# Fourteen drives by token instead of seven in a state-space scan, and rows of B spread ahead of other work on TensorE

## The chip, the cores and the metric

The kernel runs on one core of a Trainium2 chip. The metric is the device time of one launch in microseconds (us). A core has five engines with a queue of instructions each: TensorE (PE; its weight loads are listed as PEld), VectorE (DVE), ScalarE (ACT), GpSimd (POOL) and SyncE (SP), which here only starts DMA transfers. The engines wait for each other by semaphores, and each works its own queue strictly in order. PSUM, the memory that TensorE writes, has 8 banks of 128 x 512 f32.

## The reference

The input is x, 2 sequences of 1024 tokens with 128 values. The layer is a Mamba block with a residual and a layer norm, then a mixture of 8 experts (top 2, limited capacity) with a residual and a layer norm. The part around the change is the recurrence of the Mamba block, with 256 channels d and 16 states n:

```python
xz = x @ W_in;  x_in, z = split(xz, 2)
u  = silu(causal_conv4(x_in) + conv_b)
B, C = split(u @ W_x, 2)                    # 16 values each per token
dt = softplus(u @ W_dt + b_dt)
h[t] = exp(dt[t] * A) * h[t-1] + (dt[t] * u[t]) * B[t]     # state [256, 16]
y[t] = sum_n h[t, :, n] * C[t, n]
y = (y + u * D) * silu(z);  x1 = layernorm(x + y @ W_out)
# then: logits = x1 @ w_g, top 2 of 8 experts, ranks by a running count,
# rows gathered by expert, gelu(rows @ c_fc) @ c_proj, weighted, added back,
# second layernorm
```

## The kernel before

The 2048 tokens are cut into four chunks of 512 (q = 0 to 3), and a chunk has 16 units, one for each state n. A unit is numbered U = 16 q + n, 0 to 63. Channels lie on the 128 partitions in two halves d = 0 and 1. For a unit the kernel needs:

- the decay exp(dt * A[n]), made by ScalarE into PSUM banks 4 and 5 (`decays`, line 1067), once the scan of the unit before has read the bank;
- the drive dt * u * B[n]. In the usual way TensorE spreads row n of B over all partitions by a matmul with a selector (`spread_b`, line 648) into one of two banks, and VectorE multiplies it with dtu = dt * u (`drives`, line 1633);
- the scan itself, two instructions on VectorE, one per half (`scan`, line 1662);
- the product with C on GpSimd (`multiply`, line 1425), and its sum over n, added up in PSUM by TensorE (`add_to_y`, line 678 in chunks 0 to 2, where the sum is a transpose in accumulation, line 673 in chunk 3).

Seven units, listed in `TURNED` (line 54), get their drive in another way, by token: dtu, transposed beforehand so that tokens lie on the partitions (`dtu_t`), is scaled by a column of the transposed B (`b_t`) in four instructions of ScalarE (`drive_by_token`, line 1099, queued three units ahead), and eight 128 x 128 transposes of TensorE (`turn_drive`, line 664, two groups of four) bring it back to channels in the two banks that rows of B use. VectorE then has no multiplication for that unit: its scan reads PSUM directly. The decay of such a unit goes to SBUF in one instruction (`decay_sb`, line 1062). Four of the seven lie in chunk 0 (units 4, 7, 10, 14), three in chunk 3 (53, 57, 60).

State has a ring of three buffers, so the scan of unit U waits for the product of U - 3. VectorE runs each unit as: scan of half 0, the drive of the next unit, scan of half 1, then small work of the routing. Each engine's order is written out by hand. TensorE's loop (lines 820 to 880) runs for unit U: `spread_b` of the drive that VectorE makes during U (that of U + 1, or of U + 2 if U + 1 is turned), the sums of U - 2, transposes of a turned unit, and then a piece of work ("job") for another chunk: convolution, the B/C and dt projections of the next chunk, z, and for the chunk before y transposed, the output projection (`project_out`, lines 757 to 774) and the counting of experts. Jobs share PSUM banks 6 and 7 in the fixed order of `JOBS` (line 391); a job waits until ScalarE has taken the one before it in its bank. In unit n = 3 of chunks 1 to 3 TensorE waits until VectorE has gated the y of the chunk before (`gate`, line 1669), and then starts the new sum (`start_y`, lines 622 to 633). `share` on VectorE (line 1750) waits for a denominator of the routing which GpSimd makes (line 1481).

After unit 63 come the routing of the last chunk, the scatter of rows to their experts, the experts and the second norm; nothing in that part is touched.

Of the kernel before, what the change touches and what calls it, by code (L numbers as in the profile page):

```python
# [14 lines left out]
P = 128  # L15
# [38 lines left out]
TURNED = (4, 7, 10, 14, 53, 57, 60)  # L54
# [32 lines left out]
def layer_program(nc, x, W_in, channel_values, conv_rows, W_x, W_dt, A_log, W_out, w_g, c_fc, c_proj, out):  # L87
    with ExitStack() as ctx:
# [64 lines left out]
        b_t = sb("b_t", [P, TPC, D_STATE])  # L153
# [232 lines left out]
        def last_tile(e, s):  # L386
# [5 lines left out]
                ("z2a", 1), ("z2b", 0), ("wout", 1), ("wcat", 0),  # L392
                ("bc2", 1), ("dt2a", 0), ("dt2b", 1), ("y0a", 0), ("y0b", 1), ("out0a", 0), ("out0b", 1), ("conv3a", 0), ("rank0", 1),
                ("conv3b", 0),
                ("bc3", 1), ("dt3a", 0), ("dt3b", 1), ("y1a", 0), ("y1b", 1), ("out1a", 0), ("out1b", 1), ("rank1", 1),
# [137 lines left out]
        def _(pe):  # L533
# [199 lines left out]
            def turn_w_out():  # L733
                bank, made = job_bank("wout")
                pe.wait_ge(w_late_loaded, 32)
                pe.wait_ge(center_made, 1)
                for k in range(DT):
                    nc.tensor.transpose(psum[:, bank, k * P:(k + 1) * P], w_out_sb[:, k, :], ident[:, :])
                nc.tensor.matmul(psum[:, bank, DT * P:DT * P + N_EXP], center[:, 0:D_MODEL], w_g_sb[:, :], start=True, stop=True).then_inc(made, 1)
# [17 lines left out]
            def project_out(q, pair):  # L757
                for d in "ab":
                    turned, before = JOB[f"y{q}{d}"]
                    pe.wait_ge(w_taken[turned], before + 1)  # L760
                if q == 0:
                    turned, before = JOB["wcat"]
                    pe.wait_ge(w_taken[turned], before + 1)
                bank, made = job_bank(f"out{q}{'ab'[pair]}")
                b, c = divmod(q, NCH)
                for j in range(2 * pair, 2 * pair + 2):
                    for k in range(DT):
                        nc.tensor.matmul(out_tile(q, j), y_chan[:, k, j * P:(j + 1) * P], w_cat[:, k, :], start=(k == 0), stop=False)
                    t = PAD + c * CH + j * P
                    last = nc.tensor.matmul(out_tile(q, j), x_chan[:, b, t:t + P], center[:, :], start=False, stop=True)  # L770
                if q == 1 and pair == 0:
                    pe.wait_ge(bc_rows_ready, NQ)
                    turn_b(b_t_psum(bank, B_AT))
                last.then_inc(made, 1)
# [45 lines left out]
            for U in range(LAST + 1):  # L820
# [5 lines left out]
                if U in TURNED:  # L826
                    turn_drive(U, 1)
                elif U >= 1 and U - 2 not in TURNED and drive_beside(U):
                    spread_b(drive_beside(U))
# [10 lines left out]
                if U - 1 in TURNED:  # L840
                    spread_b(drive_beside(U + 1))
                if U + 1 in TURNED:
                    turn_drive(U + 1, 0)
                if q == 2 and n in (12, 14):
                    dtu_job(3, (n - 12) // 2)
                if q == 0:
# [6 lines left out]
                    elif n <= 6:  # L853
                        dt_job(1, n - 5)
                    elif n <= 10:
                        conv_job(2, (n - 7) // 2, range((n - 7) % 2 * 2, (n - 7) % 2 * 2 + 2))
                    elif n <= 12:
                        z_job(2, n - 11)
                    elif n == 13:
                        turn_w_out()  # L860
                    elif n == 15:
                        center_w_out()
                else:
# [108 lines left out]
        def _(act):  # L972
# [59 lines left out]
            def take_b(rows):  # L1032
                act.wait_ge(b_turned, 1 if rows is first_b else 2)
                if rows is not first_b:
                    act.wait_ge(drive_t_ready, TPC * sum(T < D_STATE for T in TURNED))
                nc.scalar.activation(b_t[:, :, :].rearrange("p j n -> p (j n)"), rows, ACT.Copy).then_inc(b_t_ready, 1)

            first_b = b_t_psum(B_BANK, 0)
            take_b(first_b)
# [47 lines left out]
            def drive_by_token(U):  # L1087
                q, n = divmod(U, D_STATE)
                before = TURNED.index(U)
                act.wait_ge(drive_turned, DT * before)  # L1090
                if q == 0:
                    act.wait_ge(dtu_t_ready, 1)
                    act.wait_ge(b_t_ready, 1)
                else:
                    bank, done = JOB["t3b"]
                    act.wait_ge(w_taken[bank], done + 1)
                    act.wait_ge(b_t_ready, 2)
                for j in range(TPC):
                    nc.scalar.activation(drive_t[:, j, :], dtu_t[:, j, :], ACT.Copy, scale=b_t[:, j, n:n + 1]).then_inc(drive_t_ready, 1)
# [66 lines left out]
            def take_out(q, pair):  # L1166
                act.wait_ge(logits_copied, 2 * q + pair + 1)
                rows, taken = job_made(f"out{q}{'ab'[pair]}")
                if q == 1 and pair == 0:
                    take_b(rows[:, B_AT:B_AT + TPC * D_STATE])  # L1170
# [44 lines left out]
            def take_w_out():  # L1215
                rows, taken = job_made("wout")
                nc.scalar.activation(w_out_t[:, :, :].rearrange("p k m -> p (k m)"), rows[:, 0:DT * P], ACT.Copy).then_inc(w_out_t_ready, 1)
                nc.scalar.activation(center[:, D_MODEL:WIDE], rows[:, DT * P:DT * P + N_EXP], ACT.Copy).then_inc(taken, 1)
# [7 lines left out]
            for U in range(LAST + 1):  # L1226
# [12 lines left out]
                for T in TURNED:  # L1239
                    if T - AHEAD.get(T, 2) == U:  # L1240
                        decays(T)
                    if T - 3 == U:
                        drive_by_token(T)
                if q == 2 and n in (13, 15):
# [22 lines left out]
                if q == 0:  # L1267
# [17 lines left out]
                    elif n == 14:  # L1285
                        take_w_out()
                else:
# [76 lines left out]
        def _(gp):  # L1364
# [80 lines left out]
            def times_u(q):  # L1445
                gp.wait_ge(dt_ready, DT * (q + 1))
                if q >= 2:
                    gp.wait_ge(drive_ready, drive_number(D_STATE * (q - 1)))
                    gp.wait_ge(dtu_turned, 1)
# [522 lines left out]
```

## Time and profile before

| | us |
|---|---|
| median of 3 runs | 391.63 (391.55 to 392.54) |
| profiled execution, its own time | 392.27 |
| its span, first to last instruction | 390.5 |
| VectorE busy | 290.3 |
| TensorE busy | 289.5 |
| GpSimd busy | 265.7 |
| ScalarE busy | 201.1 |

The slices of the page show the engines' busy share in tenths over 40 equal pieces of 9.8 us, and the clock that TensorE was granted (9 is full speed, 2.4 GHz; 5 is half, 1.2 GHz):

```profile
PE   8896798669686768675854799766089999998700
DVE  2699889999999999969999999995212333334566
ACT  2858987946635694753564647661302223332405
POOL 4506789968778899887889886897520555556622
PEclk9999999998788857969565699999579999999955
```

The first two slices are the start. Slices 3 to 27 are the 64 units, and what follows is routing of the last chunk and the experts.

### The profile page before, as it was taken

To read this page: it belongs to the slowest core of one execution; us is meant where nothing else is said; L and a number is where in the kernel's file an instruction comes from. 1 tells how busy PE (TensorE), PEld (TensorE's weight loads), DVE (VectorE), ACT (ScalarE), POOL (GpSimd) and SP (SyncE) were. 2 spreads that over 40 slices of the span, in tenths; PEclk is the share of its full clock that TensorE was granted. 3 is DMA by queue.
4 is the path that set the end of the run, shared out by engine and by line. 5 is a ranking of instruction groups with operands and counts; after the bars stand their busy time and mean duration, and the time that the engine had idled before them with its cause. 6 is when DMAs were issued, how large, how long until landed. Compare 5 with 4: busy or idle time off the path is not lost. (4 is left out here: it accounts for less than half of the span.)

```text
span 390.5 us, 4954 instructions
## 1 busy us (share of the span) xinstructions
PE 289.5 (74%) x1493; PEld 205.0 (53%) x1493; DVE 290.3 (74%) x436; ACT 201.1 (51%) x398; POOL 265.7 (68%) x226
## 2 busy tenths in 40 slices
PE   8896798669686768675854799766089999998700
PEld 6455455537564454564542464324088888887600
DVE  2699889999999999969999999995212333334566
ACT  2858987946635694753564647661302223332405
POOL 4506789968778899887889886897520555556622
PEclk9999999998788857969565699999579999999955
DMA  7061087462333254221212231001053434332773
GB/s 221 12 220 54 2 274 257 127 216 88 144 107 134 81 163 146 68 70 51 104 60 74 82 114 55 1 14 41 31 143 82 116 114 125 93 89 71 212 223 112
DMA packets 35786, 42.90 MB, mean 110 GB/s; under 512 B 3862, under 2 KB 26331, under 8 KB 35760
## 3 DMA queue, kind: packets, MB, share of 16 engines
q1 hardware_dynamic: 32336, 37.38, 30.8%
q0 software_dynamic: 2304, 4.24, 3.3%
q10 hardware_dynamic: 1120, 0.97, 0.9%
q8 instruction: 12, 0.20, 0.2%
q14 instruction: 14, 0.11, 0.1%
HBM read 30.11 MB, written 12.79 MB: 110 GB/s over the span
## 5 line engine op out<-in xcount | busy, mean ns | idle before, releaser
L1425 POOL TENSOR_TENSOR product<-state,c_wide 128x1024 f32<-128x1024 f32 x64 | 149.6, 2344 | 45.0 <-DVE state L1662 29.0
L1067 ACT ACTIVATE psum<-dt,a_neg 128x512 f32<-128x512 f32 x110 | 75.1, 687 | 79.3 <-DVE state L1662 77.9
L678 PE MATMUL psum<-ident,product 128*128 128x128 f32 x384 | 61.4, 313 | 33.3 <-POOL product L1425 33.3
L678 PEld LDWEIGHTS psum<-ident,product 128*128 128x128 f32 x384 | 51.2, 162 | 49.5 <-POOL product L1425 46.1
L1633 DVE TENSOR_TENSOR drive<-dtu,psum 128x1024 f32<-128x1024 f32 x57 | 68.3, 1198 | 7.3 <-PE psum L648 7.1
L1662 DVE TENSOR_TENSOR_SCAN state<-psum,carry,drive 128x512 f32<-128x512 f32 x58 | 72.2, 1268 | 0.2
L1662 DVE TENSOR_TENSOR_SCAN state<-psum,drive 128x512 f32<-128x512 f32 x56 | 66.7, 1210 | 2.5 <-ACT psum L1067 2.3
L1547 POOL DMA_INDIRECT result_rows<-state,result_at x30 | 30.3, 1011 | 40.4 <-DVE state L1876 33.1
L1501 POOL DMA_INDIRECT slot_rows<-sent,scatter_at x32 | 32.9, 1029 | 10.6 <-issue 6.8
L904 PE MATMUL psum<-product,fc_sb 128*128 128x320 f32 x128 | 36.1, 435 | 1.1 <-DVE product L1844 1.1
L1841 DVE TENSOR_SCALAR tags<-c_wide 128x10 f32<-128x10 f32 x8 | 1.3, 164 | 43.1 <-PE psum L893 43.1
L1326 ACT ACTIVATE u<-psum 128x640 f32<-128x640 f32 x16 | 11.3, 704 | 38.3 <-PE psum L904 37.2
L673 PE MATMUL psum<-product,ident 128*128 128x512 f32 x60 | 28.3, 599 | 2.7 <-POOL product L1425 2.6
L904 PEld LDWEIGHTS psum<-product,fc_sb 128*128 128x128 f32 x128 | 22.8, 190 | 11.3 <-issue 2.2
L1326 ACT ACTIVATE z_tok<-psum 128x640 f32<-128x640 f32 x16 | 11.3, 704 | 27.6 <-PE psum L904 18.9
L648 PE MATMUL psum<-bc_parts,selector 128*128 128x512 bf16 x57 | 24.5, 432 | 0.7 <-DVE drive L1633 0.7
L723 PE MATMUL psum<-x_chan,w_conv 128*128 128x512 f32 x48 | 23.9, 624 | 1.4 <-ACT sent L1172 1.1
L673 PEld LDWEIGHTS psum<-product,ident 128*128 128x128 f32 x60 | 10.7, 190 | 15.2 <-issue 9.5
L957 PE MATMUL psum<-ident 128*128 128x128 f32 x52 | 8.1, 332 | 10.7 <-DMA slot_rows<-sent,scatter_at 10.7
L578 PE MATMUL psum<-u,w_dt_sb 128*128 128x512 f32 x24 | 13.0, 668 | 3.8 <-ACT bc_parts L1112 2.7
L1876 DVE TENSOR_TENSOR state<-psum,result_weight 128x640 f32<-128x640 f32 x6 | 4.9, 824 | 14.4 <-PE psum L917 14.4
L1551 POOL DMA_INDIRECT late_rows<-state,result_at x10 | 10.6, 1064 | 5.9 <-DVE state L1872 4.1
(256 smaller groups left out, 513.2 us busy)
## 6 DMA issues: line engine op xcount, KB each, us to landing
c_wide<-c_rows SPq DMA_DIRECT2D x32, 512.0 KB, 4.0
slot_rows<-blank SPq DMA_DIRECT2D x8, 325.0 KB, 4.7
c_wide<-slot_rows SPq DMA_DIRECT2D x8, 325.0 KB, 3.3
result_rows<-zeros SPq DMA_DIRECT2D x8, 256.0 KB, 5.0
late_rows<-zeros SPq DMA_DIRECT2D x8, 256.0 KB
fc_sb<-in_c_fc SPq DMA_DIRECT2D x8, 256.0 KB
proj_sb<-in_c_proj SPq DMA_DIRECT2D x8, 256.0 KB
c_wide<-result_rows SPq DMA_DIRECT2D x8, 256.0 KB
```

Source lines behind the costliest of these rows:

```text
L648: nc.tensor.matmul(psum[:, b_bank(U), :], selector[:, n, :], bc_parts[:, q * CH:(q + 1) * CH], start=True, stop=True).then_inc(b_spread, 1)
L673: nc.tensor.matmul(psum[:, Y_BANK + d, :], ident[:, :], product[:, i, d, :], start=False, stop=True, skip_group_check=True).then_inc(summe ...
L678: last = nc.tensor.matmul(y_part(j, d), product[:, i, d, j * P:(j + 1) * P], ident[:, :], is_transpose=True, start=False, stop=True, skip_ ...
L723: last = nc.tensor.matmul(psum[:, bank, :], w_conv[:, k, d * P:(d + 1) * P], x_of(q, k), start=(k == 0), stop=(k == D_CONV - 1))
L904: last = nc.tensor.matmul(psum[:, 2 + 2 * (h % 2) + s, 0:HALF], fc_sb[:, i, h * P:(h + 1) * P], rows_chan[:, i, s * HALF:(s + 1) * HALF], ...
L1067: nc.scalar.activation(psum[:, A_BANK + d, :], dt[:, q % 2, d, :], ACT.Exp, scale=a_neg[:, n:n + 1]).then_inc(decay_ready, 1)
L1326: nc.scalar.activation(hidden[e % 2][:, h, :].rearrange("p (s k) -> p s k", s=2), psum[:, 2 + 2 * (h % 2):4 + 2 * (h % 2), 0:HALF], ACT.Ge ...
L1425: nc.gpsimd.tensor_tensor(product[:, U % PRODUCTS, channels, :], state[:, U % RING, channels, :], wide, ALU.mult).then_inc(product_ready, 1)
L1501: gp.indirect_dma_start(out=slot_rows, out_offset=bass.IndirectOffsetOnAxis(ap=scatter_at[:, k, j:j + 1], axis=0), in_=sent[:, k, j, :], i ...
L1547: gp.indirect_dma_start(out=result_rows, out_offset=bass.IndirectOffsetOnAxis(ap=result_at[:, i, s:s + 1], axis=0), in_=rows_out[:, i, s, ...
L1633: nc.vector.tensor_tensor(drive[:, drive_number(U) % 2, :, :], dtu[:, q % 2, :, :], psum[:, b_bank(U), :].unsqueeze(1).to_broadcast([P, DT ...
L1662: nc.vector.tensor_tensor_scan(state[:, U % RING, d, :], decay, rows, before, ALU.mult, ALU.add).then_inc(scanned, 1)
```

## The change

Fourteen units are turned instead of seven, four each in chunks 0, 1 and 3 and two in chunk 2. `b_t` has two buffers, and B is transposed once per chunk: for chunk 1 in the job of `turn_w_out`, for chunks 2 and 3 in the output projection of the chunk two before. dtu of chunks 1 and 2 is transposed in four new jobs (t1a, t1b, t2a, t2b), taken by ScalarE. On TensorE the spreading of a row of B moves from the head of a unit to behind the sums of the unit before it, ahead of that unit's job; only behind a turned unit it stays at the head. `center_w_out` moves from unit 15 to unit 16. GpSimd's `times_u` gets a wait for the last transposes of dtu.

```diff
-TURNED = (4, 7, 10, 14, 53, 57, 60)
+TURNED = (4, 7, 10, 14, 19, 22, 26, 29, 43, 46, 51, 54, 57, 60)
...
-        b_t = sb("b_t", [P, TPC, D_STATE])
+        b_t = sb("b_t", [P, 2, TPC, D_STATE])
...
-                ("z2a", 1), ("z2b", 0), ("wout", 1), ("wcat", 0),
+                ("z2a", 1), ("z2b", 0), ("wout", 1), ("t1a", 0), ("t1b", 1), ("wcat", 0),
...
-                ("bc3", 1), ("dt3a", 0), ("dt3b", 1), ("y1a", 0), ("y1b", 1), ("out1a", 0), ("out1b", 1), ("rank1", 1),
+                ("bc3", 1), ("dt3a", 0), ("dt3b", 1), ("y1a", 0), ("y1b", 1), ("t2a", 0), ("t2b", 1), ("out1a", 0), ("out1b", 1), ("rank1", 1),
...
@@ turn_w_out, TensorE
+                pe.wait_ge(bc_rows_ready, 2)
+                turn_b(b_t_psum(bank, B_AT))
@@ project_out, TensorE
-                if q == 1 and pair == 0:
-                    pe.wait_ge(bc_rows_ready, NQ)
+                if q <= 1 and pair == 0:
+                    pe.wait_ge(bc_rows_ready, q + 3)
                     turn_b(b_t_psum(bank, B_AT))
@@ the loop over units, TensorE
                 if U in TURNED:
                     turn_drive(U, 1)
-                elif U >= 1 and U - 2 not in TURNED and drive_beside(U):
+                elif U - 1 in TURNED and drive_beside(U):
                     spread_b(drive_beside(U))
...
                 for k in SUMS[q].get(n, []):
                     add_to_y(q * D_STATE + k)
-                if U - 1 in TURNED:
+                if U not in TURNED and U < LAST and drive_beside(U + 1):
                     spread_b(drive_beside(U + 1))
                 if U + 1 in TURNED:
                     turn_drive(U + 1, 0)
+                if q == 2 and n in (6, 7):
+                    dtu_job(2, n - 6)
...
-                    elif n == 15:
+                    elif n >= 14:
+                        dtu_job(1, n - 14)
+                else:
+                    if q == 1 and n == 0:
                         center_w_out()
-                else:
@@ ScalarE
-            def take_b(rows):
-                act.wait_ge(b_turned, 1 if rows is first_b else 2)
-                if rows is not first_b:
-                    act.wait_ge(drive_t_ready, TPC * sum(T < D_STATE for T in TURNED))
+            def take_b(q, rows):
+                act.wait_ge(b_turned, q + 1)
+                if q >= 2:
+                    act.wait_ge(drive_t_ready, TPC * sum(T < D_STATE * (q - 1) for T in TURNED))
...
+                if q == 2 and n in (6, 7):
+                    take_dtu(2, n - 6)
...
                         take_w_out()
+                    if n >= 14:
+                        take_dtu(1, n - 14)
@@ times_u, GpSimd
-                    gp.wait_ge(dtu_turned, 1)
+                    if q == 2:
+                        gp.wait_ge(dtu_turned, 1)
+                    else:
+                        for half in "ab":
+                            bank, before = JOB[f"t{q - 2}{half}"]
+                            gp.wait_ge(w_made[bank], before + 1)
```

## Rows read from the trace of the kernel before

**Rows 1.** Busy time by stretch (chunks 0 to 3, rest): PE, PEld, DVE, ACT, POOL, clock.

```profile
24.00:79.50 55.50, 44.06 (x244) 30.05 (x243) 51.15 (x45) 45.13 (x83) 42.70 (x20) 1.00 0.47 157
79.50:141.50 62.00, 46.02 (x227) 31.27 (x226) 60.61 (x76) 36.63 (x68) 49.32 (x36) 0.83 0.40 129
141.50:205.40 63.90, 44.49 (x228) 33.10 (x227) 58.81 (x77) 36.41 (x80) 54.97 (x42) 0.74 0.26 89
205.40:263.00 57.60, 43.88 (x150) 22.35 (x148) 56.26 (x72) 35.16 (x69) 49.58 (x39) 0.85 0.18 58
263.00:390.50 127.50, 90.69 (x579) 75.75 (x579) 50.47 (x151) 34.79 (x78) 59.27 (x58) 0.88 0.39 111
```

**Rows 2.** Waits of VectorE, 24 to 264 us: total, times, longest.

```profile
DVE drive L1633 <- PE psum L648: 7.1, 8, 3.5
DVE state L1662 <- ACT psum L1067: 2.3, 5, 0.7
```

**Rows 3.** Groups by line and form: busy us, mean ns, idle before.

```profile
L1633 DVE TENSOR_TENSOR drive<-dtu,psum 128x1024 f32<-128x1024 f32 x57 | 68.3, 1198 | 7.3 <-PE psum L648 7.1
...
L648 PE MATMUL psum<-bc_parts,selector 128*128 128x512 bf16 x57 | 24.5, 432 | 0.7 <-DVE drive L1633 0.7
...
L1099 ACT ACTIVATE drive_t<-dtu_t,b_t 128x256 f32<-128x256 f32 x28 | 11.9, 494 | 0.0
...
L664 PE MATMUL psum<-ident,drive_t 128*128 128x128 f32 x56 | 8.2, 275 | 0.1
```

**Rows 4.** VectorE in order of time, chunks 1 to 3: start, us, idle before.

```profile
107.27 1.22 DVE L1633 TENSOR_TENSOR drive<-dtu,psum 128x1024 f32<-128x1024 f32 x1 [0.70 <-PE psum L648]
108.41 2.45 DVE L1662 TENSOR_TENSOR_SCAN state<-psum,carry,drive 128x512 f32<-128x512 f32 x2
...
150.43 1.22 DVE L1633 TENSOR_TENSOR drive<-dtu,psum 128x1024 f32<-128x1024 f32 x1 [0.63 <-PE psum L648]
...
175.34 1.22 DVE L1633 TENSOR_TENSOR drive<-dtu,psum 128x1024 f32<-128x1024 f32 x1 [3.52 <-PE psum L648]
...
198.40 0.18 DVE L1750 RECIPROCAL denom<-denom 128x4 f32<-128x4 f32 x1 [0.45 <-POOL denom L1481]
...
222.65 1.22 DVE L1633 TENSOR_TENSOR drive<-dtu,psum 128x1024 f32<-128x1024 f32 x1 [0.95 <-PE psum L648]
```

**Rows 5.** The same of chunk 0: a drive behind turned unit 7.

```profile
54.38 1.22 DVE L1633 TENSOR_TENSOR drive<-dtu,psum 128x1024 f32<-128x1024 f32 x1 [0.42 <-PE psum L648]
```

**Rows 6.** All engines in order of time, around unit 19.

```profile
87.24 0.58 ACT L1111 ACTIVATE bc_sb<-psum 128x512 f32<-128x512 f32 x1
...
88.36 3.11 PE L578 MATMUL psum<-u,w_dt_sb 128*128 128x512 f32 x4 [1.91 <-ACT bc_parts L1112]
...
91.69 2.34 PE L632 MATMUL psum<-diag_d,u 128*128 128x128 f32 x16
...
96.03 1.22 DVE L1633 TENSOR_TENSOR drive<-dtu,psum 128x1024 f32<-128x1024 f32 x1 [0.18 <-PE psum L648]
```

**Rows 7.** GpSimd in order of time, units 25 to 27.

```profile
118.19 2.37 POOL L1425 TENSOR_TENSOR product<-state,c_wide 128x1024 f32<-128x1024 f32 x1 [1.38 <-issue]
...
130.63 0.20 POOL L1481 TENSOR_TENSOR denom<-denom,others 128x4 f32<-128x4 f32 x1
```

**Rows 8.** All engines in order of time, units 39 to 41.

```profile
170.02 1.97 PE L678 MATMUL psum<-ident,product 128*128 128x128 f32 x8 [2.22 <-POOL product L1425]
...
174.91 0.39 PE L648 MATMUL psum<-bc_parts,selector 128*128 128x512 bf16 x1
...
175.14 1.04 PE L678 MATMUL psum<-ident,product 128*128 128x128 f32 x8
...
177.83 2.36 POOL L1425 TENSOR_TENSOR product<-state,c_wide 128x1024 f32<-128x1024 f32 x1 [3.25 <-issue]
```

**Rows 9.** TensorE in order of time, units 51 and 52.

```profile
217.08 1.97 PE L754 MATMUL psum<-ident,z_tok 128*128 128x128 f32 x8 [5.17 <-DVE z_tok L1669]
...
218.84 3.56 PE L625 MATMUL psum<-u,diag_d 128*128 128x512 f32 x4
```

More of the change, by code:

```diff
@@ L1029, in _ @@
                     nc.scalar.activation(bc_sb[:, :], psum[:, B_BANK + 1, :], ACT.Copy).then_inc(bc_rows_ready, 1)
-            def take_b(rows):
-                act.wait_ge(b_turned, 1 if rows is first_b else 2)
-                if rows is not first_b:
-                    act.wait_ge(drive_t_ready, TPC * sum(T < D_STATE for T in TURNED))
-                nc.scalar.activation(b_t[:, :, :].rearrange("p j n -> p (j n)"), rows, ACT.Copy).then_inc(b_t_ready, 1)
-            first_b = b_t_psum(B_BANK, 0)
-            take_b(first_b)
+            def take_b(q, rows):
+                act.wait_ge(b_turned, q + 1)
+                if q >= 2:
+                    act.wait_ge(drive_t_ready, TPC * sum(T < D_STATE * (q - 1) for T in TURNED))
+                nc.scalar.activation(b_t[:, q % 2, :, :].rearrange("p j n -> p (j n)"), rows, ACT.Copy).then_inc(b_t_ready, 1)
+            take_b(0, b_t_psum(B_BANK, 0))
             copy_x(3)
@@ L1090, in drive_by_token @@
                 act.wait_ge(drive_turned, DT * before)
+                act.wait_ge(b_t_ready, q + 1)
                 if q == 0:
                     act.wait_ge(dtu_t_ready, 1)
-                    act.wait_ge(b_t_ready, 1)
                 else:
-                    bank, done = JOB["t3b"]
-                    act.wait_ge(w_taken[bank], done + 1)
-                    act.wait_ge(b_t_ready, 2)
+                    job_taken(f"t{q}a")
+                    job_taken(f"t{q}b")
                 for j in range(TPC):
-                    nc.scalar.activation(drive_t[:, j, :], dtu_t[:, j, :], ACT.Copy, scale=b_t[:, j, n:n + 1]).then_inc(drive_t_ready, 1)
+                    nc.scalar.activation(drive_t[:, j, :], dtu_t[:, j, :], ACT.Copy, scale=b_t[:, q % 2, j, n:n + 1]).then_inc(drive_t_ready, 1)
             def job_made(name):
@@ L1168, in take_out @@
                 rows, taken = job_made(f"out{q}{'ab'[pair]}")
-                if q == 1 and pair == 0:
-                    take_b(rows[:, B_AT:B_AT + TPC * D_STATE])
+                if q <= 1 and pair == 0:
+                    take_b(q + 2, rows[:, B_AT:B_AT + TPC * D_STATE])
                 tiles = slice(TPC * q + 2 * pair, TPC * q + 2 * pair + 2)
@@ L1217, in take_w_out @@
                 nc.scalar.activation(w_out_t[:, :, :].rearrange("p k m -> p (k m)"), rows[:, 0:DT * P], ACT.Copy).then_inc(w_out_t_ready, 1)
+                take_b(1, rows[:, B_AT:B_AT + TPC * D_STATE])
                 nc.scalar.activation(center[:, D_MODEL:WIDE], rows[:, DT * P:DT * P + N_EXP], ACT.Copy).then_inc(taken, 1)
```

## The prediction

> **What bounds the kernel now.** I read the page's slices first, then the busy time of each chunk, then the waits of VectorE, then the order of time where it waits. The slices show VectorE at nine tenths in nearly all of slices 3 to 27, which are the 64 units. The stretches [rows 1] say how close: VectorE is busy 51.15 of 55.5 us in chunk 0, 60.61 of 62.0 in chunk 1, 58.81 of 63.9 in chunk 2 and 56.26 of 57.6 in chunk 3. The 127.5 us behind them are not touched by the change and only shift. GpSimd comes next and is the engine to watch: 49.32 of 62.0 in chunk 1, but 54.97 of 63.9 in chunk 2. What VectorE waits for inside the units is little: 7.1 us for TensorE's spread rows of B, 2.3 us for decays [rows 2]. So there are two things to win, work on VectorE and the 7.1 us, and about 9 us of GpSimd idle time in chunk 2 to win it in.
>
> **Part 1: drives leave VectorE.** Unit 53 goes back to the usual way, eight units leave it, net seven: four in chunk 1 (19, 22, 26, 29), two in chunk 2 (43, 46), one in chunk 3. A drive lasts 1.20 us [rows 3] but overlaps its neighbour: the one that starts at 107.27 is followed by a scan at 108.41, 1.14 us later, a wait before it included or not [rows 4]. I take 1.13. Upper end: 7 x 1.13 = 7.9 us. Lower end: see the first rival.
>
> **Part 2: the same work on ScalarE and TensorE.** ScalarE gets 7 x 4 = 28 scalings more, at 11.9 / 28 = 0.43 us each beside each other [rows 3] 1.7 us per unit, 12 us in all, and four dtu copies, two copies of B. It is busy 36.63 of 62.0 and 36.41 of 63.9 us in chunks 1 and 2 [rows 1], and its jobs lie between two decays. The decays of a unit must be there 3.4 us (two scans, one drive) after the last ones could start, so a job of 1.7 us fits beside 1.3 us of decays, and behind a turned unit there is a whole unit more, because the decay of the unit after it needs only the scan before it. I count nothing for ScalarE; if that cover is gone the price is a few tenths at a unit, up to 7 x 0.5 = 3.5 us. TensorE gives a spread (0.43) and takes eight transposes (8.2 / 56 = 0.15 each, 1.2 per unit) [rows 3]: 7 x 0.7 = 5 us, and some 5 us for the dtu and B transposes. It has 16 and 19 us idle in chunks 1 and 2 [rows 1], so it costs only where something is queued behind.
>
> **Part 3: the spread in front of the job.** Behind the sums of unit U TensorE now spreads B for the drive of U + 2. It needs the drive of U done (it shares a bank), and that ends about when the product of U - 2 does, on which the sums wait, so I charge no new wait. What it skips are jobs. In chunks 1 to 3 five waits are long [rows 4, 6]: 0.18 (behind two sums and `start_y`), 0.70 (behind an output projection), 0.63 (behind the B/C projection), 3.52 (behind sums and an output projection) and 0.95 (behind y transposed and `start_y`). The waits of 0.70 and 0.63 go whole. Those of 0.18 and 0.95 don't, since `start_y` and not a job is ahead of them. In chunk 0 nothing goes: its waits, such as the 0.42 at 54.38 [rows 5], stand behind turned units, where the spread stays at the head of the unit, behind the job.
>
> The wait of 3.52: the sums start at 170.02 and wait for GpSimd, last 1.77 at the low clock, then comes the projection until the spread at 174.91 [rows 8]. In the new order the spread runs at 171.8 and the drive can start at 172.2 instead of 175.34, 3.1 us earlier. But the projection and the new job t2b (four transposes at the low clock, 1.0 us) are now behind it, and the spread after them waits for both: 171.8 + 0.4 + 1.0 + 2.9 (the projection) + 1.0 (sums, as at 175.14) + 0.4 = 177.5 at the low clock, 176.5 if the clock rises at 174.4 as it did. VectorE would want its drive at 175.8 (172.2 + drive + two scans). So 0.7 us comes back as a wait, and chunk 2 keeps 2.3 to 2.4; I take 2.3.
>
> **Part 4: chunk by chunk.**
> Chunk 1, unit 19. This is where it is tight. TensorE's queue is now: dt projection of half b, second group of transposes of 19, gate wait, `start_y`, two sums, and only then the row for the drive of 21. The projection waits for ScalarE's bc rows, which end later by the new decay and scaling (87.24 [rows 6], about 1.0 us later). Before, `start_y` began at 91.69 and the drive at 96.03; VectorE now wants that drive 1.1 us earlier, and TensorE has it at best at 95.6 (clock high) and at worst at 98 (the projection at the low clock lasts 3.11, the transposes 1.0). Between +0.4 and -2; I take -0.5. Units 22, 26 and 29 give 1.13 each, and 0.70 from part 3: 4.1, less 0.5 is 3.6. Now the cap: from the product of unit 25 at 118.19 GpSimd works without a gap (times_u, score, products) until the denominator at 130.63 [rows 7], for which VectorE's `share` in unit 28 waits. This chain of 12.6 us starts earlier only by what was won until unit 25, which is -0.5 + 1.13 + 0.70 = 1.3; the gain of 26 is lost there, that of 29 comes behind it. Chunk 1 gives 1.3 + 1.13 = 2.4 us.
> Chunk 2: 0.6 + 2.3 = 2.9 us until unit 41. Then the same chain of GpSimd; in this chunk VectorE already waits 0.45 us for it [rows 4], so unit 43's 1.13 is lost, and unit 46's comes behind it: 1.1. GpSimd can follow, its gap of 3.25 us at 177.83 [rows 8] is the twin of the 3.52. Chunk 2 gives 4.0 us.
> Chunk 3: one drive less, but the turned unit is now 51, the one with `start_y`. There TensorE is bound by the gate: 8 transposes from 217.08, `start_y` from 218.84 until 222.4 [rows 9], both at the low clock, then the row. VectorE reaches it one drive earlier and waits 2.1 instead of 0.95: 0 us, and up to 2 if the clock is high there (`start_y` 3.56 then takes half).
>
> Sum: 2.4 + 4.0 + 0 = 6.4 us. The profiled execution took 392.27 us (span 390.5), so 385.9; it lies 0.64 above the median 391.63, which gives **385.2 us**.
>
> **The rivals.**
> *Every turned unit brings its own wait.* For it: chunk 0 has four turned units and 55.5 - 51.15 = 4.35 us of VectorE idle [rows 1], about 1.09 per unit, nearly what a drive costs; chunk 1 without any has 1.39. Against it: in chunk 0 ScalarE is busy 45 of 55 us, in chunks 1 and 2 it is 36 of 62. The time: 7 x (1.13 - 1.09) = 0.3 and 0.70 + 0.63 + 2.3 of the reorder, 3.9 less: 387.7.
> *Nothing else takes the place.* All 7.9 us, and all waits for TensorE of chunks 1 to 3, 0.18 + 0.70 + 0.63 + 3.52 + 0.95 = 6.0: 377.7. For it: GpSimd has 12.7 and 8.9 us of room. Against it: the gap-free chain of GpSimd [rows 7].
> *The low clock makes TensorE the bound* (the slower side). A sum takes 1.97 us at the low clock and 1.04 at the high one [rows 8]. In chunks 1 and 2 TensorE is busy 46.02 + 44.49 = 90.5 us at a mean clock of 0.83 and 0.74, about 71 us at the full clock, and some 8 more now. At the low clock throughout that is 158 us in stretches that lasted 126: sums arrive late, the ring of state stops VectorE. It decides from a mean clock of 79 / 126 = 0.63 down; at 0.60 the two stretches last 132 instead of 126, at 396 to 398 us, less what chunk 3 gives. For it: the clock already fell from 0.83 to 0.74 as gaps of 2 to 3 us before the sums grew, and a matmul of 512 columns is replaced by transposes. Against it: TensorE gets more work and shorter gaps.
> The Trainium skill (TensorE: Matmul & The Clock Gate, Part 4: PE-mode transpose) says that transposes don't count as busy for the clock in the way matmuls do. The trace leans that way: chunks 1 and 2, where the sums are transposes, have 0.83 and 0.74, chunk 3 with matmul sums 0.85 [rows 1]; but chunk 0, full of transposes between projections, has 1.00. By that rule the clock would fall with this change and the third rival's time would hold; I don't follow it, because the trace's low stretches go with idle gaps.
>
> **How the numbers follow.** The forecast 0.50, nothing takes its place 0.12, each unit its own wait 0.20, the low clock 0.12, and 0.06 for a mixture that ends at no change. The range: 380.5 (part of the second rival's way) to 391.0 (all new waits of unit 19 and ScalarE's 3.5 us, 6.4 - 1.5 - 3.5 = 1.4 less, and a margin), which leaves out most of the full and of the slow case. Changes under 0.3%, 1.2 us, can't be told from none. Faster 0.50 + 0.12 + 0.18 = 0.80, same 0.06 + 0.02 = 0.08, slower 0.12.
>
> **What would show it.** Right: VectorE's wait at the drive of unit 41 falls from 3.5 to under 1, the ones of 0.70 and 0.63 are gone, `share` waits 1 us or more for GpSimd in chunks 1 and 2, and the drives behind units 19 and 51 wait 1 to 2 us for TensorE. GpSimd is nearly without gaps in chunk 2. Wrong: waits of 0.5 us or more behind 22, 26, 29, 43 and 46 (the first rival); a clock under 0.65 in chunks 1 and 2 (the third); unit 19 costing over 2 us; or decays late at units 20 to 30.

## The result, and the profile after

The changed kernel takes **384.55 us** in the median of 4 runs (384.05 to 386.32), against 391.59 us (390.65 to 392.54) before: ratio 0.9841, interval 0.9809 to 0.9873. That is 7.0 us less; the forecast was 6.4 less, at 385.2. The profiled execution took 384.32 us with a span of 382.6.

The stretches come first, cut where the chunks now end. Columns as in [rows 1].

```profile
79.50:137.90 58.40, 43.05 (x263) 31.39 (x262) 55.97 (x73) 42.25 (x82) 49.42 (x36) 0.96 0.44 139
137.90:196.90 59.00, 41.40 (x253) 32.60 (x251) 56.53 (x75) 39.78 (x88) 55.14 (x42) 0.87 0.29 95
196.90:255.10 58.20, 45.18 (x154) 24.15 (x152) 55.33 (x71) 36.42 (x72) 49.52 (x39) 0.85 0.17 57
255.10:382.60 127.50, 91.10 (x579) 76.20 (x579) 50.59 (x151) 34.78 (x78) 59.53 (x58) 0.88 0.38 111
```

Against [rows 1]: the part behind the units has kept its 127.5 us, and so has chunk 0 its 55.5 (not shown; the first scan of unit 16 starts 0.03 us earlier than before). Chunk 1 lasts 58.4 instead of 62.0, chunk 2 59.0 instead of 63.9, chunk 3 58.2 instead of 57.6. Take VectorE's busy time off each length and the gain falls into two parts:

| chunk | VectorE busy | VectorE idle | sum |
|---|---|---|---|
| 1 | 60.61 to 55.97, -4.64 | 1.39 to 2.43, +1.04 | -3.6 |
| 2 | 58.81 to 56.53, -2.28 | 5.09 to 2.47, -2.62 | -4.9 |
| 3 | 56.26 to 55.33, -0.93 | 1.34 to 2.87, +1.53 | +0.6 |

Over the three, busy time gives 7.85 us, seven drives at 1.12, and idle time gives 0.05. That reads as if the new order had done nothing. VectorE's waits, 24 to 256 us, say why it does not mean that (total, times, longest):

```profile
DVE drive L1649 <- PE psum L648: 4.5, 7, 1.2
DVE denom L1766 <- POOL denom L1497: 2.8, 2, 1.6
DVE state L1678 <- ACT psum L1074: 2.3, 5, 0.7
```

The waits for spread rows fell from 7.1 to 4.5 us [rows 2], and the waits for GpSimd's denominator rose from 0.45 [rows 4] to 2.8. What was won on the waits for spread rows (2.6 us) went into the waits for the denominators (2.4 us). ScalarE's 2.3 us did not move.

The groups by line and form (busy, mean ns, idle before) answer to [rows 3]:

```profile
L1649 DVE TENSOR_TENSOR drive<-dtu,psum 128x1024 f32<-128x1024 f32 x50 | 60.0, 1199 | 4.6 <-PE psum L648 4.5
...
L648 PE MATMUL psum<-bc_parts,selector 128*128 128x512 bf16 x50 | 20.0, 404 | 2.0 <-DVE state L1678 1.5 <-DVE drive L1649 0.5
...
L1105 ACT ACTIVATE drive_t<-dtu_t,b_t 128x256 f32<-128x256 f32 x56 | 23.7, 494 | 1.0 <-PE psum L664 0.9
...
L664 PE MATMUL psum<-ident,drive_t 128*128 128x128 f32 x112 | 18.7, 296 | 8.6 <-DVE drive L1649 7.6 <-ACT drive_t L1105 1.0
```

50 drives instead of 57, 56 scalings instead of 28 and 112 transposes instead of 56. A drive and a scaling last what they did, a transpose 296 ns instead of 275 and a spread 404 instead of 432. The transposes now stand 7.6 us behind drives on VectorE. That is idle time of TensorE; no wait of VectorE is put down to a transpose (line 664) in this trace.

VectorE in order of time (start, us, idle before) answers to [rows 4, 6]:

```profile
95.58 1.22 DVE L1649 TENSOR_TENSOR drive<-dtu,psum 128x1024 f32<-128x1024 f32 x1 [0.89 <-PE psum L648]
...
128.26 0.18 DVE L1766 RECIPROCAL denom<-denom 128x4 f32<-128x4 f32 x1 [1.23 <-POOL denom L1497]
...
154.34 1.22 DVE L1649 TENSOR_TENSOR drive<-dtu,psum 128x1024 f32<-128x1024 f32 x1 [0.38 <-PE psum L648]
...
167.81 1.19 DVE L1649 TENSOR_TENSOR drive<-dtu,psum 128x1024 f32<-128x1024 f32 x1
...
190.84 0.18 DVE L1766 RECIPROCAL denom<-denom 128x4 f32<-128x4 f32 x1 [1.58 <-POOL denom L1497]
...
213.22 1.22 DVE L1649 TENSOR_TENSOR drive<-dtu,psum 128x1024 f32<-128x1024 f32 x1 [1.17 <-PE psum L648]
...
220.65 1.28 DVE L1678 TENSOR_TENSOR_SCAN state<-decay_sb,carry,psum 128x512 f32<-128x512 f32 x1 [0.37 <-issue]
...
223.92 1.22 DVE L1649 TENSOR_TENSOR drive<-dtu,psum 128x1024 f32<-128x1024 f32 x1 [0.82 <-PE psum L648]
...
255.15 1.91 DVE L1835 TENSOR_TENSOR product<-state,c_wide 128x512 f32<-128x512 f32 x1
```

The waits of 0.70 and 0.63 are gone. The 3.52 us one is gone whole: 167.81 is the drive of unit 41, without a wait. The 0.18 has become 0.89 and the 0.95 has become 1.17. New are 1.23 and 1.58 us at the denominators of chunks 1 and 2, and in chunk 3 the waits at 220.65 and 223.92, at turned unit 54 and behind it.

The last row is the mark by which the experiments are read. It is VectorE's last product of the units; before, it started at 263.07:

```profile
263.07 1.91 DVE L1819 TENSOR_TENSOR product<-state,c_wide 128x512 f32<-128x512 f32 x1
```

It now starts 7.92 us earlier, and what is behind it lasts as long as before in this execution. But the time from the start of the trace to the first scan of unit 0 isn't fixed: it is 24.97 us before, 24.91 in the changed kernel and 24.2 to 25.0 in the experiments, though none of them edits what comes ahead of it. So the mark is counted from that scan. It comes 238.10 us behind it before and 230.24 in the changed kernel. Below, **gain** is how much less than 238.10 us lie between the first scan of unit 0 and the mark, and "gain at unit U" is the same for U's first scan. The whole times scatter more, since the part from the mark to the end took between 126.5 and 131.4 us in the profiled executions. In the changed kernel the gain at unit 16 is 0.0, at 21 0.4, at 24 2.3, at 30 3.6, at 41 7.5, at 46 7.5, at 48 8.5 and at the mark 7.9.

### The profile page after: what moved, and what is told of

Its sections match the earlier page's. It is cut to its first block and busy times, and to the rows that moved or that the text cites. A ratio compares the mean times of both kernels' runs of the same rounds, so it can differ in the third digit from the quotient of the medians.

```text
span 382.6 us, 5173 instructions
## 1 busy us (share of the span) xinstructions
PE 286.2 (75%) x1566; PEld 207.6 (54%) x1566; DVE 282.6 (74%) x429; ACT 211.8 (55%) x425; POOL 266.2 (70%) x226
## 5 line engine op out<-in xcount | busy, mean ns | idle before, releaser
L1074 ACT ACTIVATE psum<-dt,a_neg 128x512 f32<-128x512 f32 x96 | 65.0, 686 | 53.1 <-DVE state L1678 51.8
L678 PE MATMUL psum<-ident,product 128*128 128x128 f32 x384 | 56.1, 295 | 24.5 <-POOL product L1436 24.5
L1678 DVE TENSOR_TENSOR_SCAN state<-psum,drive 128x512 f32<-128x512 f32 x52 | 62.0, 1212 | 2.5 <-ACT psum L1074 2.3
L1649 DVE TENSOR_TENSOR drive<-dtu,psum 128x1024 f32<-128x1024 f32 x50 | 60.0, 1199 | 4.6 <-PE psum L648 4.5
L1678 DVE TENSOR_TENSOR_SCAN state<-psum,carry,drive 128x512 f32<-128x512 f32 x48 | 60.0, 1269 | 0.2
L664 PE MATMUL psum<-ident,drive_t 128*128 128x128 f32 x112 | 18.7, 296 | 8.6 <-DVE drive L1649 7.6
L1105 ACT ACTIVATE drive_t<-dtu_t,b_t 128x256 f32<-128x256 f32 x56 | 23.7, 494 | 1.0 <-PE psum L664 0.9
L664 PEld LDWEIGHTS psum<-ident,drive_t 128*128 128x128 f32 x112 | 14.4, 152 | 16.1 <-issue 14.3
L648 PE MATMUL psum<-bc_parts,selector 128*128 128x512 bf16 x50 | 20.0, 404 | 2.0 <-DVE state L1678 1.5
L1678 DVE TENSOR_TENSOR_SCAN state<-decay_sb,carry,psum 128x512 f32<-128x512 f32 x16 | 19.6, 1261 | 0.4 <-issue 0.4
```

Source lines behind the costliest of these rows:

```text
L664: last = nc.tensor.transpose(psum[:, turned_bank(U, d), j * P:(j + 1) * P], drive_t[:, j, d * P:(d + 1) * P], ident[:, :])
L678: last = nc.tensor.matmul(y_part(j, d), product[:, i, d, j * P:(j + 1) * P], ident[:, :], is_transpose=True, start=False, stop=True, skip_ ...
L1074: nc.scalar.activation(psum[:, A_BANK + d, :], dt[:, q % 2, d, :], ACT.Exp, scale=a_neg[:, n:n + 1]).then_inc(decay_ready, 1)
L1649: nc.vector.tensor_tensor(drive[:, drive_number(U) % 2, :, :], dtu[:, q % 2, :, :], psum[:, b_bank(U), :].unsqueeze(1).to_broadcast([P, DT ...
L1678: nc.vector.tensor_tensor_scan(state[:, U % RING, d, :], decay, rows, before, ALU.mult, ALU.add).then_inc(scanned, 1)
```

## The experiments

Theory: the gain is drives off VectorE plus the waits that the new order removes; GpSimd's chain to each denominator caps the first, `start_y` the rest. Rivals: each turned unit brings a wait of its own; or one of the two halves of the change did it all.

**Order alone.** Only the new order, jobs and tiles, with the seven turned units of before.

```diff
-TURNED = (4, 7, 10, 14, 19, 22, 26, 29, 43, 46, 51, 54, 57, 60)
+TURNED = (4, 7, 10, 14, 53, 57, 60)
```

> The changed kernel with the seven turned units of before: the new place of the spreads (and the transposes of dtu and B, now unused) without the seven further turned units. My theory: the place of the spreads removes VectorE's waits of 0.70, 0.63 and 3.52 us at the drives of units 24, 35 and 41, which is 4.2 us when nothing comes back behind unit 41 (there the changed kernel shows nothing), so about 387.5 us, 4.1 less than before. Rival, the jobs that the spreads now pass are late in their turn and the wait only moves: 0 to 1.5 us, 390 to 391.6.

Measured: 387.07 us, ratio 0.988 (0.9855 to 0.9905); gain 4.8, at unit 24 1.1, at 41 4.8. What is left of the waits, with the last product:

```profile
166.63 1.22 DVE L1649 TENSOR_TENSOR drive<-dtu,psum 128x1024 f32<-128x1024 f32 x1 [0.44 <-PE psum L648]
...
217.62 1.22 DVE L1649 TENSOR_TENSOR drive<-dtu,psum 128x1024 f32<-128x1024 f32 x1 [0.95 <-PE psum L648]
...
258.06 1.91 DVE L1835 TENSOR_TENSOR product<-state,c_wide 128x512 f32<-128x512 f32 x1
```

The 3.52 at the drive of unit 41 is gone; the 0.44 stands at the drive of unit 40, and 0.20 at a decay behind it. The 0.18 is gone too. The 0.95 stands as in [rows 4], as does the 0.45 at the denominator, which is 0.44 here: with no drives taken away, the denominators are no later for VectorE than before.

**Turned units alone.** The fourteen units, with the spread where it was.

```diff
-                elif U - 1 in TURNED and drive_beside(U):
+                elif U >= 1 and U - 2 not in TURNED and drive_beside(U):
                     spread_b(drive_beside(U))
...
-                if U not in TURNED and U < LAST and drive_beside(U + 1):
+                if U - 1 in TURNED:
                     spread_b(drive_beside(U + 1))
```

> The changed kernel with the spreads where they were (head of the unit), so the fourteen turned units alone. My theory: units 22, 29 and 46 bring 1.13 us each, 19 about 0.4, 26 and 43 nothing (GpSimd's chain), 51 nothing, and the waits of 0.70, 0.63 and 3.52 stay: 3 to 4 us less than before, 388 us. Rival, each turned unit brings a wait of its own as in chunk 0 and only the place of the spreads makes them pay: 0 to 1 us, 391.

Measured: 387.06 us (384.9 to 390.6), 0.9892 (0.9861 to 0.9924); gain 2.8. VectorE's rows:

```profile
128.04 0.18 DVE L1766 RECIPROCAL denom<-denom 128x4 f32<-128x4 f32 x1 [1.23 <-POOL denom L1497]
...
171.58 1.22 DVE L1649 TENSOR_TENSOR drive<-dtu,psum 128x1024 f32<-128x1024 f32 x1 [3.14 <-PE psum L648]
...
194.64 0.18 DVE L1766 RECIPROCAL denom<-denom 128x4 f32<-128x4 f32 x1 [1.58 <-POOL denom L1497]
218.11 1.22 DVE L1649 TENSOR_TENSOR drive<-dtu,psum 128x1024 f32<-128x1024 f32 x1 [2.26 <-PE psum L648]
```

Seven drives left VectorE, 7.9 us of work, and 2.8 came out. Most of the rest is in these rows, and 1.2 us is at unit 54 and behind it. The wait of 0.70, which the expectation left standing, is gone here as well. The two halves give 4.8 + 2.8 = 7.6, together 7.9, so neither did it all. By chunk they are not so separate: in chunk 1 the turned units alone give 3.5, the order alone 1.3 and both 3.7; in chunk 2 it is 0.8, 3.5 and 4.8 (4.5 in the repeated run below). So chunk 1 owes its gain to the turned units and chunk 2 mostly to the order.

**Without units 26 and 43**, whose gain the forecast called lost in GpSimd's chain.

```diff
-TURNED = (4, 7, 10, 14, 19, 22, 26, 29, 43, 46, 51, 54, 57, 60)
+TURNED = (4, 7, 10, 14, 19, 22, 29, 46, 51, 54, 57, 60)
```

> The changed kernel without turned units 26 and 43 (twelve). My theory: what these two save is lost where VectorE waits 1.23 and 1.58 us for GpSimd's denominator in units 28 and 45, so the time stays within 0.5 us of the changed kernel's 384.5 and the two waits shrink to 0.1 and 0.5 us. Rival, each turned unit is worth its 1.13 us: 386.8.

Measured: 387.49 us, 0.9911 (0.9876 to 0.9947); gain 6.7, at unit 48 8.1. In its profiled execution:

```profile
127.50 0.18 DVE L1766 RECIPROCAL denom<-denom 128x4 f32<-128x4 f32 x1
...
190.47 0.18 DVE L1766 RECIPROCAL denom<-denom 128x4 f32<-128x4 f32 x1 [0.44 <-POOL denom L1497]
```

The wait of 1.23 is gone and the 1.58 is down to 0.44: each is the drive that was taken away, come back as a wait. Chunks 1 and 2 gain 3.5 and 4.6 us with two drives more on VectorE, against 3.7 and 4.8 (3.7 and 4.5 in the repeated run): up to unit 48 the two turned units are worth 0.0 to 0.4 us, as the theory has it. Chunk 3 loses 1.4 us instead of 0.6 or 0.3, with the wait behind unit 51 at 1.78; what sets that wait follows below. The median did not meet what the theory expected of it: by the ratios (0.9911 against 0.9841 and 0.9852) it lies 2.3 to 2.7 us above the changed kernel, which is the rival's figure. So the rows settle where the two drives went; that the whole time doesn't need the two units is not shown.

**The shares of the experts later**, one unit in chunks 1 and 2, so that VectorE has other work while GpSimd makes the denominator.

```diff
-        SHARE = [0, 12, 13, 11]
-        PLACE = [0, 13, 14, 12]
+        SHARE = [0, 13, 14, 11]
+        PLACE = [0, 14, 15, 12]
```

> The changed kernel with VectorE's reciprocal and GpSimd's weights one unit later in chunks 1 and 2 (and so the scatter too). My theory: both waits for the denominator go, but GpSimd is nearly full behind them, so that only a part of 2.8 us comes: 0.5 to 1.5 us less than the changed kernel, 383 to 384. Rival A, the reciprocal is the cap and not GpSimd: 2.3 to 2.8 us less, 382. Rival B, the scatter one unit later hits GpSimd's work of the next chunk: no gain or a loss, 384.5 to 386.

Measured: 386.08 us, 0.987 (0.9846 to 0.9893); gain 7.0, at unit 48 8.1. The expected gain didn't come. The waits for the denominator are gone, and in their place stands this one (VectorE, then ScalarE, in order of time):

```profile
135.20 1.28 DVE L1678 TENSOR_TENSOR_SCAN state<-psum,carry,drive 128x512 f32<-128x512 f32 x1 [2.06 <-ACT psum L1074]
```

```profile
133.25 1.30 ACT L1062 ACTIVATE psum<-dt,a_neg 128x512 f32<-128x512 f32 x2 [2.50 <-DVE sent L1808]
```

The decays of unit 32 wait 2.50 us for the bank that VectorE gives back only behind `sent`, which had moved with the share. The gain is 4.3 at unit 30 and 2.1 at unit 32. Chunk 2 gains 6.0, 1.2 to 1.5 more than without the edit, which makes up for most of it.

Beside the next three experiments **the changed kernel ran once more**.

> The changed kernel itself, beside the other runs of this call. My theory and every rival: 384.5 us, within 1 us.

Measured: 385.81 us (385.26 to 386.78), 0.9852 (0.9824 to 0.9879); gain 7.8, 0.1 less than in its first profile, while its median is 1.3 us higher. That the two gains lie so close is in part luck: chunk 2 gives 4.5 instead of 4.8 and chunk 3 loses 0.3 instead of 0.6. The experiment with chunk 3 as it was, further below, has the changed kernel's code in chunk 2 and gains 3.9 there. So a difference of less than 1 us between two gains is put down to an edit below only where a wait shows it.

One source of this scatter shows in the traces. Behind `start_y` in chunk 3 VectorE waits for a row of B, and the wait follows the length of `start_y`, the same instructions in each run. With unit 51 turned and the new order, seven executions have `start_y` at 2.37, 2.64, 2.82, 3.24, 3.33, 3.39 and 3.62 us and the wait at 0.90, 1.17, 1.36, 1.78, 1.86, 1.92 and 2.17: the wait is the length less 1.46 us, within 0.01. With 53 turned instead, five have 3.01, 3.11, 3.39, 3.55 and 3.56 us and 0.41, 0.50, 0.78, 0.95 and 0.95: the length less 2.6 us. The mean granted clock within `start_y` is 0.79 in the shortest and 0.51 in the longest. The difference of the two constants, 1.15 us, is one drive: however long `start_y` takes, the drive that unit 51 takes off VectorE comes back whole as a wait.

**The shares later in chunk 2 alone**:

```diff
-        SHARE = [0, 12, 13, 11]
-        PLACE = [0, 13, 14, 12]
+        SHARE = [0, 12, 14, 11]
+        PLACE = [0, 13, 15, 12]
```

> The changed kernel with the reciprocal, the weights and the scatter one unit later in the third chunk only (chunk 2), where no decay of unit 32 waits for the same bank. My theory: the wait of 1.58 us for GpSimd's denominator goes, 0.9 us or so of it stays won until unit 48 (as in the run with both chunks, from unit 35 to 48), 383.6. Rival, GpSimd is full behind it or its scatter runs into the next chunk: no gain, 384.5 or more.

Measured: 385.28 us, 0.9824 (0.9796 to 0.9851); gain 6.9, at unit 48 8.4, against 8.5 and 8.1 without the edit. The wait of 1.58 at the denominator is gone; 0.69 of it comes back at `sent`, as a wait for GpSimd's weight, and units 40 to 42 wait 1.1 us, where the changed kernel's two profiles wait 0.4 and 0.6 in units 36 to 41. The rest is lost behind 51, where the wait is 2.17: `start_y` lasts 3.62 us here. A miss: nothing clear is won in chunk 2, and what is lost in chunk 3 goes by the clock within `start_y`.

**The new order behind turned units too**, where the spread had stayed at the head of the unit.

```diff
-                elif U - 1 in TURNED and drive_beside(U):
-                    spread_b(drive_beside(U))
...
-                if U not in TURNED and U < LAST and drive_beside(U + 1):
+                if U < LAST and drive_beside(U + 1):
```

> The changed kernel with the spread ahead of the job behind turned units as well (at the tail of the turned unit, behind a wait for its first scan). My theory: the waits of 0.45, 0.42, 0.32 and 0.82 us behind turned units 4, 7, 10 and 54 go, 1 to 2 us less than the changed kernel; those behind 19 and 51 stay, since start_y and not a job is ahead of them. Rival, TensorE stands at the spread until the turned unit's scan and its jobs are late, which ScalarE and VectorE then wait for: 0 or slower, 384.5 to 386.

Measured: **383.37 us** (381.96 to 384.66), 0.9787 (0.9756 to 0.9818); gain 9.4, 1.6 more than the changed kernel, 1.0 of it in chunk 0. The waits of chunk 0 behind turned units (0.42 in [rows 5]) and the 0.82 behind unit 54 are gone. Those behind 19 and 51 (0.89 and 1.36), which stand behind `start_y` and not behind a job, stay, as do the two at the denominators.

**Chunk 3 as it was**, with 53, 57, 60 instead of 51, 54, 57, 60.

```diff
-TURNED = (4, 7, 10, 14, 19, 22, 26, 29, 43, 46, 51, 54, 57, 60)
+TURNED = (4, 7, 10, 14, 19, 22, 26, 29, 43, 46, 53, 57, 60)
```

> The changed kernel with chunk 3's turned units as before (53, 57, 60 in place of 51, 54, 57, 60), thirteen in all. My theory: turned unit 51 is worth nothing, as its drive is given back at the wait for the gate and start_y: within 0.5 us of the changed kernel. Rival, it is worth its 1.13 us: 385.6.

Measured: 386.10 us, 0.9848 (0.9808 to 0.9888); gain 7.8, with a drive more on VectorE. The row behind `start_y` is

```profile
214.37 1.22 DVE L1649 TENSOR_TENSOR drive<-dtu,psum 128x1024 f32<-128x1024 f32 x1 [0.50 <-PE psum L648]
```

Chunk 3 gains 0.4 instead of losing 0.6 (0.3 in the repeated run), a difference of 0.8 to 1.0 us. `start_y` flatters the changed kernel in this: it lasts 3.11 us here and 2.64 and 2.37 there. Taken at the 3.56 us that it lasted before, chunk 3 comes to 0.0 here and to 1.5 lost in both profiles of the changed kernel, so the move to 51 and 54 costs 1.5 us (an estimate from these rows). The rows show 1.2 of it at unit 54 and behind it. The whole time doesn't show it; the part behind the mark took 131.4 us in this execution, against 127.4, and chunk 2 gave 0.6 to 0.9 less.

**GpSimd's chain begun a unit earlier.** Only the unit in which it forms dt times u moves.

```diff
-                    elif n == (11 if q == 0 else 8 + q):
+                    elif n == (11 if q == 0 else 7 + q):
                         times_u(q + 1)
```

> The changed kernel with GpSimd's product dt * u (times_u) one unit earlier in chunks 1 and 2, so that it fills a gap of 1.2 and 0.9 us and leaves the chain of GpSimd in front of VectorE's share. My theory, that this chain takes the gain of turned units 26 and 43: the waits of 1.23 and 1.58 us shrink to 0.1 and 0.6, and the last scan starts 1.5 to 2 us earlier than in the changed kernel (252.6), at 250.6 to 251.1. Rival, GpSimd is full as a whole, so that the product is only late somewhere else (the ring of state): no change, 252.6.

Measured: **382.08 us** (381.38 to 385.28), 0.981 (0.977 to 0.985); gain 9.4, 1.5 to 1.6 more than the changed kernel. Up to unit 48 it is 10.6, 2.1 to 2.4 more; `start_y` at 3.39 us, with a wait of 1.92 behind it, takes the rest back. GpSimd in order of time, first in the changed kernel, then here:

```profile
115.61 2.36 POOL L1436 TENSOR_TENSOR product<-state,c_wide 128x1024 f32<-128x1024 f32 x1 [1.18 <-issue]
117.93 2.35 POOL L1466 TENSOR_TENSOR dtu<-dt,u 128x1024 f32<-128x1024 f32 x1
...
128.02 0.21 POOL L1497 TENSOR_TENSOR denom<-denom,others 128x4 f32<-128x4 f32 x1
```

```profile
113.93 2.39 POOL L1466 TENSOR_TENSOR dtu<-dt,u 128x1024 f32<-128x1024 f32 x1
116.25 4.78 POOL L1436 TENSOR_TENSOR product<-state,c_wide 128x1024 f32<-128x1024 f32 x2
...
126.45 0.20 POOL L1497 TENSOR_TENSOR denom<-denom,others 128x4 f32<-128x4 f32 x1
```

In the changed kernel GpSimd idles 1.18 us and then works without a gap for 12.6 us, as in [rows 7]. Here `dtu` fills that idle time and the denominator is there 1.57 us earlier, 0.39 of which is the earlier start of unit 0 in this execution; the 1.18 left is the idle time. The wait of 1.23 is gone, that of 1.58 is 0.6. That is the cap shown directly: nothing of the work was taken away, its place alone was changed.

**Two, then all three together.** First the order behind turned units with chunk 3 as it was:

> The spread ahead of the job behind turned units too, with chunk 3's turned units as before (53, 57, 60). From the two runs with one of these each: the last scan starts 2.1 us (1.2 in chunk 0 and 0.8 behind unit 54) or, with 54 gone, 1.2 and 1.0 us, together 2.0 to 2.3 us earlier than in the changed kernel's 252.6: 250.4. Rival, both removed the same wait: 251.4.

Measured: 384.85 us, 0.985 (0.9814 to 0.9887); gain 9.8, 1.9 to 2.0 more than the changed kernel where 2.0 to 2.3 was expected and 1.2 by the rival. That is close to the first. Chunk 0 gives 1.0 of it and not the expected 1.2, which had the earlier start of unit 0 in it.

And with `times_u` earlier as well:

> Both and the earlier times_u: if each is separate, the last scan starts at about 248.7 and the time is 381.5 us; if GpSimd or ScalarE becomes the bound before that, 250 and 383.

Measured: **381.18 us** (378.82 to 382.31), **0.9754** (0.9724 to 0.9785), the best of all; gain 11.8, 4.0 more than the changed kernel, so neither GpSimd nor ScalarE became the bound. VectorE's waits in its units:

```profile
DVE state L1675 <- ACT psum L1071: 2.3, 5, 0.7
DVE drive L1646 <- remote: 1.2, 2, 0.9
...
DVE drive L1646 <- PE psum L648: 0.8, 1, 0.8
DVE denom L1763 <- POOL denom L1494: 0.6, 1, 0.6
```

Rows for drives cost 2.0 us (1.2, whose releaser the trace leaves unnamed, and 0.8) instead of 4.5, the denominators 0.6 instead of 2.8.

## Why the prediction was right, step by step

**Part 1, the drives.** Right: 7.9 us forecast, 7.85 us of VectorE's busy time.

**Part 2, ScalarE and TensorE at nothing.** Right for ScalarE, which got 5.6 and 3.4 us more in chunks 1 and 2 while VectorE's waits for it stayed at 2.3 us. For TensorE it holds in chunks 1 and 2: no wait appeared behind 22, 26, 29, 43 or 46. So the first rival (387.7) is out for these five. It holds for unit 54, which brought 0.37 and 0.82 us of waits, as much as its drive.

**Part 3, the order.** The waits of 0.70 and 0.63 went, as forecast, though the 0.70 goes with the turned units alone as well. At unit 41 2.3 of 3.5 us were to be kept, and 3.5 were. The term that was mis-sized is the 0.7 us that "comes back as a wait" since "the spread after them waits for both", priced at the low clock. TensorE there now:

```profile
165.60 1.09 PE L678 MATMUL psum<-ident,product 128*128 128x128 f32 x8 [1.83 <-POOL product L1436]
166.53 0.38 PE L648 MATMUL psum<-bc_parts,selector 128*128 128x512 bf16 x1
166.75 0.60 PE L716 MATMUL psum<-ident,dtu 128*128 128x128 f32 x4
```

The order is the one forecast: sums, spread, then the job (the projection follows it). But eight sums last 1.09 us and not the 1.97 of [rows 8], the four transposes 0.60 and not the 1.0 I had put in, so the next spread was in time. The clock, not the queue, was mis-set, and which clock stands there changes from run to run. In the experiment with chunk 3 as it was, the same sums run at the low one:

```profile
165.18 1.97 PE L678 MATMUL psum<-ident,product 128*128 128x128 f32 x8 [0.90 <-POOL product L1436]
```

There VectorE waits 1.2 us at units 40 to 42 (0.38 for a row of B, 0.82 for decays); in the repeated run of the changed kernel it is 0.6. So at the low clock something of the forecast's size does come back. In the first profile the extra is 1.2 us, of which 0.4 went to a wait at 154.34 that the forecast had not.

**Part 4, chunk 1: 2.4 forecast, 3.7 measured.** Unit 19 was to lose 0.5 and gave 0.4. The same misjudged clock:

```profile
88.26 0.57 ACT L1117 ACTIVATE bc_sb<-psum 128x512 f32<-128x512 f32 x1
...
89.37 1.98 PE L578 MATMUL psum<-u,w_dt_sb 128*128 128x512 f32 x4 [1.13 <-ACT bc_parts L1118]
91.19 0.60 PE L664 MATMUL psum<-ident,drive_t 128*128 128x128 f32 x4
91.63 1.95 PE L632 MATMUL psum<-diag_d,u 128*128 128x128 f32 x16
```

`bc_sb` is 1.02 us later than in [rows 6], as forecast (1.0), and the projection starts 1.01 later. It then lasts 1.98 instead of 3.11, so `start_y` still begins at 91.63, where it was at 91.69. The drive behind it starts 0.45 earlier, in spite of its wait of 0.89. The other 0.3 us lie in the chunk's other units and were not traced. The wait of 0.89 is just under the 1 us that the forecast gave as a sign of being right. The cap was right in place and price: 1.13 lost, a wait of 1.23, gone in both experiments that touch it, with unit 26 back on VectorE and with the chain earlier. In every run that leaves GpSimd's order and the share alone the chain lasts 12.6 us.

**Chunk 2: 4.0 forecast, 4.8 measured** (4.5 in the repeated run); 1.2 more at unit 41, less the wait at 154.34. The cap was right here too (43 worth nothing, a wait of 1.58). GpSimd is busy 55.14 of 59.0 us, nearly gapless as forecast.

**Chunk 3: 0 forecast, 0.6 lost.** The wait behind 51 is 1.17 us, not 2.1. TensorE:

```profile
208.56 1.97 PE L756 MATMUL psum<-ident,z_tok 128*128 128x128 f32 x8 [1.13 <-DVE z_tok L1685]
210.32 2.64 PE L625 MATMUL psum<-u,diag_d 128*128 128x512 f32 x4
212.80 0.38 PE L648 MATMUL psum<-bc_parts,selector 128*128 128x512 bf16 x1
```

`start_y` takes 2.64 instead of 3.56 [rows 9], since the granted clock rises within it (0.50 from 210.3 to 211.6, 0.91 from 211.6 to 213.0). By the rule of the seven executions above a `start_y` of 3.56 would have left a wait of 2.10, the forecast's 2.1: the mechanism of unit 51 was right, and the clock was the unknown. What the forecast left out is unit 54: 0.37 at it and 0.82 behind it, both gone with chunk 3 as it was. With `start_y` as long as it was before, chunk 3 would have lost 1.5 us where 0 was forecast; the clock, which the forecast had allowed to give up to 2 us, gave back 0.9.

**The rivals.** "Nothing takes the place" (377.7) is out: it wanted 13.9 us, and VectorE still waits 4.5 us for rows of B and 2.8 for the denominators. "The low clock makes TensorE the bound" (396 to 398) is out. By each stretch's mean clock, the low level took (1 - 0.83) x 2 x 62 + (1 - 0.74) x 2 x 63.9 + (1 - 0.85) x 2 x 57.6 = 72 us of chunks 1 to 3 before, and 38 us by the same sum now. The Trainium skill (TensorE: Matmul & The Clock Gate, Part 4: PE-mode transpose) says that transposes don't count as busy for the clock as matmuls do. By that rule the clock should have fallen with the turned units. The trace doesn't agree: in the experiment with them alone it was 0.96 in chunk 1 and 0.82 in chunk 2, against 0.83 and 0.74 before. VectorE's units are shorter there too, so this shows that the forecast by that rule fails here, not what transposes count for.

In the units the forecast of 6.4 us is 1.5 under the 7.9 of the profiled execution: 1.3 too low in chunk 1, 0.8 in chunk 2, 0.6 too high in chunk 3. Against the medians it is 0.6 under 7.0, which is partly luck: misses of both signs cancel in it, and the repeated run's median gives 5.6, which puts it 0.8 over.

## What to carry to other kernels

Work taken off the busiest engine is worth its time only up to the next thing that engine waits for. Before removing it, find for each stretch the chain of another engine with no gap in it, and count from where that chain starts: here two of seven drives came back as two waits of their own size. Moving that chain's start one unit earlier, an edit of one digit, gave 2.1 to 2.4 us up to the end of the chunks that it touches, about two drives, and 1.5 to 1.6 us at the mark; taking the order change to the units it had left out gave 1.6. Count a mark inside the program from another mark inside it, since the start of the trace moved by up to 0.8 us here. Splitting the idle time per stretch into who ended it shows such an exchange; a total of idle time, the same before and after, hides it.

## What the runs showed of the hardware

TensorE's granted clock went up with more transposes in the same time: 0.96 and 0.87 in chunks 1 and 2 (0.81 for chunk 2 in the repeated run) against 0.83 and 0.74, and 0.99 and 0.86 in the kernel with all three edits. With the order alone, whose new jobs are transposes too, it was 0.91 and 0.75. At either level the same rows recur: eight sums 1.04 to 1.09 or 1.97 us, the dt projection 1.98 or 3.11; `start_y` of chunk 3, which mostly has the change of level within it, lies anywhere from 2.37 to 3.62. What sets the level was not isolated by any run, and since a stage's price here differs by a factor of 1.6 to 1.9 with it, a forecast should carry both.
